# First context, its keys, values and queries of layer one's cross attention, and first rows, made inside the preceding stages of a decoder kernel

## What is computed

```python
# layer zero's experts, whose result enters layer one
return x + _mlp(x, shared_wg, shared_wu, shared_wd) + expert_weighted
# layer one, self attention
qkv = (X @ W_qkv).reshape(b, s, h, d, 3)
weights = softmax(q @ k.T / sqrt(64))
out = (weights @ v).reshape(b, s, h * d) @ W_out
# layer one, cross attention
xn, cn = layer_norm(x, g1, b1), layer_norm(context, g2, b2)
q = xn @ Wq
k, v = split(cn @ Wkv)
out = softmax(q @ k.T * 64**-0.5) @ v @ Wout + bout
```

## Time and profile before

| | |
|---|---|
| runs, median (lowest to highest) | 1822.67 us (1822.57 to 1828.09) |
| the profiled execution's own time | 1826.97 us, of it 1825.3 us span |
| TensorE busy in the span | 1645.2 us, 90% |
| VectorE, ScalarE, GpSimd busy | 61%, 49%, 31% |
| stage experts_0 ends, self_attention_1 begins | about 722 to 727 us in the span |
| stage self_attention_1 ends, context_attention_1 begins | about 1070 to 1071 us |
| stage context_attention_1 ends | about 1480 us |

### The profile page before, as it was taken

How to read it: one execution, slowest core, us unless ns; L and a number is a source line. 1 busy time by engine, 2 the same in 40 slices (tenths; PEclk the granted TensorE clock), 3 DMA queues, 4 the chain that set the end, 5 groups by cost and what they waited for, 6 DMA issues and landing times. The chain is left out here.

```text
span 1825.3 us, 36539 instructions
## 1 busy us (share of the span) xinstructions
PE 1645.2 (90%) x12703; PEld 1360.2 (75%) x12703; DVE 1118.3 (61%) x2667; ACT 885.8 (49%) x2544; POOL 558.4 (31%) x864
## 2 busy tenths in 40 slices
PE   5997599999998887599999869999999989999998
PEld 3665467777776576488888757777777779999987
DVE  4776467777777433377776645667666554444464
ACT  2333255555555133155555524444444456666644
POOL 2112222444443234322221121222332256444410
PEclk8999699999999799799999979999999989999999
DMA  8000323444450353100000020000000032213001
GB/s 252 0 0 1 117 78 119 129 127 127 127 169 12 130 167 118 44 14 14 17 12 1 1 87 19 17 18 18 18 18 1 1 127 82 70 70 137 2 1 41
DMA packets 87277, 114.29 MB, mean 63 GB/s; under 512 B 4788, under 2 KB 76680, under 8 KB 86888
## 3 DMA queue, kind: packets, MB, share of 16 engines
q1 hardware_dynamic: 82008, 99.56, 16.9%
q0 software_dynamic: 5136, 12.98, 2.1%
HBM read 64.68 MB, written 47.84 MB: 62 GB/s over the span
## 5 line engine op out<-in xcount | busy, mean ns | idle before, releaser
L1029 ACT ACTIVATE c_probs<-ps,c_negmax 112x375 f32<-112x375 f32 x256 | 143.7, 581 | 2.1 <-DVE c_negmax L1135 2.1
L1240 PEld LDWEIGHTS ps<-const,c_probs 112*125 112x125 f32 x768 | 97.8, 193 | 47.3 <-DVE c_pT L1157 27.5
L1135 DVE TENSOR_REDUCE c_negmax<-ps 112x2 f32<-112x750 f32 x128 | 114.2, 934 | 25.7 <-PE ps L1271 25.7
L1240 PE MATMUL ps<-const,c_probs 112*125 112x112 f32 x768 | 116.1, 289 | 3.6 <-ACT c_probs L1029 2.4
L1988 PE MATMUL ps<-xnT,s_qkv 128*128 128x224 f32 x512 | 112.7, 370 | 4.6 <-ACT e_gate_up L1777 4.1
L1793 ACT ACTIVATE s_probs<-ps,s_negmax 112x112 f32<-112x112 f32 x256 | 86.7, 364 | 36.4 <-DVE s_negmax L1851 36.4
L1988 PEld LDWEIGHTS ps<-xnT,s_qkv 128*128 128x128 f32 x512 | 96.3, 196 | 10.8 <-ACT e_gate_up L1777 5.7
L1330 PE MATMUL ps<-parts 128*125 128x256 f32 (+1 forms) x480 | 91.0, 327 | 5.5 <-DVE X L1086 2.4
L2903 DVE TENSOR_TENSOR e_hid_low<-xnT,e_hid_high 128x528 fp32r<-128x528 f32 x56 | 41.1, 733 | 83.5 <-ACT e_hid_high L2803 83.5
L1017 ACT COPY c_pT<-ps 125x672 f32<-125x672 f32 x64 | 46.1, 720 | 82.1 <-PE ps L1240 82.1
L1330 PEld LDWEIGHTS ps<-parts 128*125 128x125 f32 (+1 forms) x480 | 71.7, 196 | 13.0 <-DVE c_kT L1081 4.4
(11 more groups left out here) (473 smaller groups left out, 5088.1 us busy)
## 6 DMA issues: line engine op xcount, KB each, us to landing
expert_rows<-d_zero SPq DMA_DIRECT2D x16, 2240.0 KB
c_ctx_in<-in_ctx SPq DMA_DIRECT2D x32, 375.0 KB
e_x_in<-expert_rows SPq DMA_DIRECT2D x43, 128.0 KB, 2.1
expert_rows<-e_y POOLq DMA_DIRECT2D x43, 128.0 KB, 2.1
e_w_gate_even<-in_L_ffn_w_gate SPq DMA_DIRECT2D x4, 1024.0 KB, 5.1
e_w_fc_even<-in_L_ffn_w_c_fc SPq DMA_DIRECT2D x4, 1024.0 KB, 7.3
e_w_proj_even<-in_L_ffn_w_c_proj SPq DMA_DIRECT2D x4, 1024.0 KB, 9.8
c_kv<-in_L_ffn_w_gate SPq DMA_DIRECT2D x4, 1024.0 KB, 5.0
```

The source lines that it names most:

```text
L1029: last = nc.scalar.activation(probs[:, g % 2, r, :], ps[:T, r, 0:S], ACT.Exp, bias=negmax[:, par, h:h + 1], accum_out=sums[:, par, h:h + 1])
L1135: nc.vector.tensor_reduce(negmax[:, par, h:h + 3:2], ps[:T, 2 * piece:2 * piece + 2, 0:S], AX.X, ALU.max, negate=True).then_inc(max_done, 1)
L1240: last = nc.tensor.transpose(ps[:KC, bank + r % 2, k * T:(k + 1) * T], probs[:, g % 2, r, k * KC:(k + 1) * KC], ident[:T, :T])
```

## The change

- A class `Wide` cuts tiles out of one memory of 8192 float32 per partition that lives from the start to the end of layer one's cross attention. Six tiles of `linear_attention` with `attnT`, three of `context_attention_0`, the weights of `self_attention_1` (queries and keys apart from values now) and the keys, values, transposed context and first queries of `context_attention_1` take turns in it.
- In `experts_0`: SyncE loads context 0 after the other loads; VectorE normalises it in ten small steps, one per tile j of 28 to 37, GpSimd takes its power at j of 33; TensorE transposes it before the last two steps; behind the last step it makes the keys of sequence 0 (8 products of 128 x 375) and the first of three value parts (2 products of 512 columns), in plain float32 instead of split products. ScalarE and VectorE copy them out. GpSimd, not SyncE, waits for all stores, and then issues the gathers of sequences 0 and 1.
- In `self_attention_1`: TensorE makes the two other value parts of context 0 first; the gathers go without a copy of the row numbers; sequence q's sum is made one iteration earlier (0 and 1 both in iteration -5), with two sets of norm tiles; contexts 1 and 2 are loaded when four sums were made; context 1, not 0, is normalised in the iterations B-3 and B-2; in the last iteration TensorE makes the first queries of the next stage (8 products of 224 columns) and ScalarE copies them out.
- In `context_attention_1`: the scores, maxima and exponentials of sequence 0 stand ahead of the iterations; the contexts, keys and values of 0 and the queries of the first pair are gone from them. Context 3 is loaded once context 1 is normalised, which it is at the start.

The diff, cut:

```diff
+class Wide:
+
+
+    SIZE = 8192
+
+    def __init__(self, memory):
+        self.memory, self.at = memory, 0
+
+    def afresh(self):
+        self.at = 0
+        return self
+
+    def __call__(self, shape):
+        n = int(np.prod(shape[1:]))
+        assert self.at + n <= self.SIZE
+        flat, self.at = self.memory[:shape[0], self.at:self.at + n], self.at + n
+        names = "abcd"[:len(shape) - 1]
+        return flat.rearrange("p (" + " ".join(names) + ") -> p " + " ".join(names), **dict(zip(names, shape[1:])))
...
-        w = sb("wqkv", [128, 2, 3 * D])
+        wide = sh.wide
+        w = wide([128, 2, 3 * D])
...
-        kT = sb("kT", [128, 2, 2, S])
-        v = sb("v", [KC, 2, NK, VROW])
-        probs = sb("probs", [T, 2, GROUPS, S])
+        wide = sh.wide.afresh()
+        kT = wide([128, 2, 2, S])
+        v = wide([KC, 2, NK, VROW])
+        probs = wide([T, 2, GROUPS, S])
...
+def gather_rows(nc, sh, w, q, u):
+
+    for k in range(2):
+        nc.gpsimd.indirect_dma_start(out=w.gathered[:, u, k, :], out_offset=None, in_=sh.xs[:, :],
+                                     in_offset=bass.IndirectOffsetOnAxis(ap=sh.kept_row[:, q, k:k + 1], axis=0)).then_inc(w.arrived[u], 16)
...
+                if j == LATER + len(later):
+                    entry.load(sp, 0, 0)
...
+                if j == CONTEXT_AT + 5:
+                    entry.power(pool, 0)
+            for u in range(IN_SLOTS):
+                pool.wait_ge(stored[u], (BLOCKS - u + IN_SLOTS - 1) // IN_SLOTS * 16)
+            pool.sem_inc(passed, 1)
+            for q in range(2):
+                gather_rows(nc, sh, following, q, q)
...
+            for m in (1, 3):
+                act.wait_ge(early_mm, m + 1)
+                nc.scalar.copy(later_w.kT[0][:, m, :], ps[:, KEY_BANKS[m], 0:S]).then_inc(early_taken, 1)
...
+                if 0 <= j - CONTEXT_AT < entry.STEPS:
+                    entry.step(dve, 0, 0, j - CONTEXT_AT)
...
+            dve.wait_ge(following.parts_ready, 16)
+            for c in range(2):
+                dve.wait_ge(ctx_mm, c + 1)
+                nc.vector.tensor_scalar(later_w.ctxT[:, c, :], ps[:, BANK_X + c, 0:S], sh.columns[:, 148 + c:149 + c],
+                                        sh.columns[:, 150 + c:151 + c], ALU.mult, ALU.add).then_inc(ctxT_ready, 1)
+            for m in (0, 2):
+                dve.wait_ge(early_mm, m + 1)
+                nc.vector.tensor_copy(later_w.kT[0][:, m, :], ps[:, KEY_BANKS[m], 0:S])
+            dve.wait_ge(early_mm, 5)
+            nc.vector.tensor_copy(later_w.v[0][:, 0, :], ps[:KC, BANK_X, :])
...
+                if j == LAST - 1:
+                    pe.wait_ge(entry.cn_ready, 1)
+                    pe.wait_ge(xT_ready, BLOCKS)
+                    for c in range(2):
+                        for k in range(NK):
+                            last = nc.tensor.transpose(ps[:, BANK_X + c, k * KC:(k + 1) * KC], entry.cn[:, k, c * 128:(c + 1) * 128], ident[:KC, :KC])
+                        last.then_inc(ctx_mm, 1)
+            pe.wait_ge(sh.w_loaded["c1"], 64)
+            pe.wait_ge(ctxT_ready, 2)
+            for m in range(4):
+                for c in range(2):
+                    last = nc.tensor.matmul(ps[:, KEY_BANKS[m], 0:S], later_w.kv[:, c, m * 128:(m + 1) * 128], later_w.ctxT[:, c, :],
+                                            start=(c == 0), stop=(c == 1))
+                last.then_inc(early_mm, 1)
+            for c in range(2):
+                last = nc.tensor.matmul(ps[:KC, BANK_X, :], later_w.ctxT[:, c, 0:KC], later_w.kv[:, c, 512:1024], start=(c == 0), stop=(c == 1))
+            last.then_inc(early_mm, 1)
...
+    STEPS = 10
+
+    def step(self, dve, q, u, n):
+        nc = self.nc
+        if n < NK:
+            if n == 0:
+                dve.wait_ge(self.loaded[u], q * 8 + 16 - 8 * u)
+                dve.sem_inc(self.passed, 1)
+            last = nc.vector.bn_stats(self.stats[:, n, :], self.ctx_in[:, u, n, :])
+            if n == NK - 1:
+                last.then_inc(self.chain, 1)
+        elif n == NK:
+            dve.wait_ge(self.chain, q * 2 + 1)
+            dve.sem_inc(self.passed, 1)
+            for j in range(NK):
+                last = nc.vector.bn_aggr(self.mv[:, j, :], self.stats[:, j, :])
+            last.then_inc(self.chain, 1)
+        elif n == NK + 1:
+            dve.wait_ge(self.chain, q * 2 + 2)
+            nc.vector.tensor_scalar(self.veps[:, :], self.mv[:, :, 1], LN_EPS, None, ALU.add).then_inc(self.var_ready, 1)
+        elif n >= self.STEPS - NK:
+            j = n - self.STEPS + NK
+            if j == 0:
+                dve.wait_ge(self.rstd_ready, q + 1)
+            last = nc.vector.tensor_scalar(self.cn[:, j, :], self.ctx_in[:, u, j, :], self.mv[:, j, 0:1],
+                                           self.rstd[:, j:j + 1], ALU.subtract, ALU.mult)
+            if j == NK - 1:
+                last.then_inc(self.cn_ready, 1)
...
+        def sums_at(i):
+
+            if i <= -AHEAD:
+                return range(2) if i == -AHEAD - 1 else ()
+            return (i + AHEAD + 1,) if within(i + AHEAD + 1) else ()
...
-            for u in range(2):
-                entry.load(sp, u, u)
+            sp.wait_ge(taken, AHEAD)
+            for q in (1, 2):
+                entry.load(sp, q, q % 2)
...
-                if not (isinstance(q, int) and q < 2):
-                    pool.wait_ge(taken, q - 1)
+                pool.wait_ge(taken, q - 1)
                 pool.sem_inc(passed_in, 1)
-                nc.gpsimd.tensor_copy(row[:, u, :], sh.kept_row[:, q, :]).then_inc(row_ready, 1)
-                pool.wait_ge(row_ready, q + 1)
-                pool.sem_inc(passed_in, 1)
-                for k in range(2):
-                    nc.gpsimd.indirect_dma_start(out=gathered[:, u, k, :], out_offset=None, in_=sh.xs[:, :],
-                                                 in_offset=bass.IndirectOffsetOnAxis(ap=row[:, u, k:k + 1], axis=0)).then_inc(arrived[u], 16)
+                gather_rows(nc, sh, w, q, u)
...
-                gather(i + AHEAD + 2, par)
+                gather(i + AHEAD + 3, 1 - par)
                 if i == B - 2:
-                    entry.power(pool, 0)
+                    entry.power(pool, 1)
...
+                if i == B:
+                    for half in range(2):
+                        act.wait_ge(query_mm, half + 1)
+                        nc.scalar.copy(later_w.qT[0][:, :, 2 * half:2 * half + 2, :].rearrange("p s m t -> p m s t"),
+                                       columns_of(ps[:, BANK_S + half, :]))
...
+            for k in range(1, NK):
+                act.wait_ge(early_mm, k)
+                nc.scalar.copy(later_w.v[0][:, k, :], ps[:KC, BANK_O + k - 1, :])
...
-                entry_sum(i, par)
+                if i >= 0:
+                    for q in sums_at(i):
+                        entry_sum(q)
...
+                if i < 0:
+                    for q in sums_at(i):
+                        entry_sum(q)
...
+            def later_queries():
+                pe.wait_ge(exp_done, 4 * B)
+                for half in range(2):
+                    for m in range(2):
+                        cols = slice((2 * half + m) * 128, (2 * half + m + 1) * 128)
+                        for c in range(2):
+                            last = nc.tensor.matmul(ps[:, BANK_S + half, 2 * m * T:2 * (m + 1) * T], later_w.q[:, c, cols],
+                                                    sh.xnT[:, c, 0:2, :].rearrange("p s t -> p (s t)"), start=(c == 0), stop=(c == 1))
+                    last.then_inc(query_mm, 1)
...
+                if i == B:
+                    later_queries()
...
+            for k in range(1, NK):
+                for c in range(2):
+                    last = nc.tensor.matmul(ps[:KC, BANK_O + k - 1, :], later_w.ctxT[:, c, k * KC:(k + 1) * KC], later_w.kv[:, c, 512:1024],
+                                            start=(c == 0), stop=(c == 1))
+                last.then_inc(early_mm, 1)
...
-    side = Side([("slots0", -3, ON_ACT), ("result", -1, ON_DVE), ("query", 2, ON_ACT), ("key0", 1, ON_DVE), ("context0", 2, ON_ACT),
-                 ("key1", 1, ON_DVE), ("key2", 1, ON_ACT), ("slots1", -3, ON_ACT),
-                 ("key3", 1, ON_DVE), ("rows_ranks", -1, ON_DVE, B + 1), ("value0", 1, ON_ACT), ("value1", 1, ON_DVE),
-                 ("context1", 2, ON_ACT), ("inverse_logits", 0, ON_DVE, B + 1), ("value2", 1, ON_ACT)])
+    side = Side([("slots0", -3, ON_ACT), ("result", -1, ON_DVE), ("query", 2, ON_ACT, B, 2), ("key0", 1, ON_DVE, B, 1), ("context0", 2, ON_ACT, B, 1),
+                 ("key1", 1, ON_DVE, B, 1), ("key2", 1, ON_ACT, B, 1), ("slots1", -3, ON_ACT),
+                 ("key3", 1, ON_DVE, B, 1), ("rows_ranks", -1, ON_DVE, B + 1), ("value0", 1, ON_ACT, B, 1), ("value1", 1, ON_DVE, B, 1),
+                 ("context1", 2, ON_ACT, B, 1), ("inverse_logits", 0, ON_DVE, B + 1), ("value2", 1, ON_ACT, B, 1)])
...
+            sp.wait_ge(cn_ready, 2)
```

(23 more changed lines are left out.)

203 lines of the change are left out of this document (106 added, 97 removed).

## The result

| | kernel before | changed kernel |
|---|---|---|
| median of the runs beside each other | 1825.38 us (4 runs, 1822.57 to 1828.60) | 1811.07 us (4 runs, 1809.45 to 1811.88) |
| ratio | | 0.9925, 95% interval 0.9908 to 0.9942 |
| the same comparison repeated | 1825.01 us (11 runs) | 1809.41 us (6 runs), 0.9917, 0.9902 to 0.9932 |
| profiled execution, span | 1826.97 us, 1825.3 | 1809.45 us, 1807.8 |

The change makes the kernel faster by 14 to 16 us. The forecast was 1804.5 us with a range up to 1811: the sign is right, the time is not. Two things are to be found: what the forecast's 18.2 us really were, and how much of the gap is the starting point of the sum.

What follows compares the result with a forecast made beforehand. TensorE was taken as the bound inside stages, so only two stage borders could gain: 14.8 and 3.4 us make 18.2, and 1822.67 less 18.2 gives 1804.5 us, range 1799 to 1811 us.

Steps and rivals of the forecast that it cites:

- starting point: Whole kernel: the time before the change, taken as a median of 1822.67 us, from which 18.2 us were subtracted.
- B: Border self_attention_1 to context_attention_1: scores start at once, the old order is reached earlier; gain 14.8 us, bounds 12 to 17.
- A: Border experts_0 to self_attention_1: second transposes follow sooner and less half clock; gain 3.4 us, bounds -1 to 7.
- ten VectorE steps ... hidden; at worst 0.3 each where the power is late: Tile loop of experts_0: steps fit VectorE's idle time; with six context transposes 0.6 us, bounds 0 to 3.
- With the barrier the next one starts at 732.9: End of experts_0: gathers end at 731.2, the barrier adds some 1.7 us, then self_attention_1 starts.
- the value products: Start of self_attention_1: two value parts on TensorE take 3.9 us at full clock, 7.6 at half.
- gathers: End of experts_0: GpSimd issues four gathers, 1.3 us each, from 726.0 to 731.2.
- keys and values: End of experts_0: TensorE's ten products take 5.7 and 1.9 us, from 722.0 to 729.6.
- rival 3: Border into context_attention_1: context 3 lands late and VectorE stands for 5 us; 1809.5 us, chance 0.04.
- rival 5: Self_attention_1 and context_attention_0: new addresses in the wide memory slow TensorE's products; 1829 us at 3.5%, chance 0.03.
- rival 4: Start of context_attention_1: the removed 22.9 us return as waits of iteration 0; 1819 us or more, chance 0.04.
- The rule weighed: Experts_0: VectorE and GpSimd share memory interfaces, so stores come later beside the new steps; gain 1 us smaller.

Runs made afterwards that it cites:

- queries_back: Changed kernel with the first queries of context_attention_1 made at that stage's start again, not inside self_attention_1: 1812.9 us (6 runs).
- power_early: Changed kernel with GpSimd's root of the first context's variances taken one tile earlier: 1804.3 us (10 runs, together with its repeat).
- gather_split: Changed kernel with only sequence 1's gathers moved from the end of experts_0 to the start of self_attention_1: 1810.9 us (6 runs).
- gather_late: Changed kernel with the gathers of sequences 0 and 1 moved from the end of experts_0 to the start of self_attention_1: 1810.6 us (6 runs).
- sums_early: Changed kernel with GpSimd's root one tile earlier and the sums of sequences 0 and 1 moved to the end of experts_0: 1804.9 us (4 runs).
- power_again: The same kernel as power_early, run once more: 1804.3 us (10 runs, both together).
- keys_back: Changed kernel with the first context's keys and first values made at the start of self_attention_1, not the end of experts_0: 1817.3 us (10 runs).

## Why the prediction was wrong, step by step

- **The starting point** (1822.67 us). The median of three runs stood for that of the kernel, and I took 4.3 us off a profiled execution that lay 1.8 above the median of 41. This made the forecast 2.5 us low. From 1825.1 the same sum gives 1806.9, inside 2.7 us of the changed kernel's 1809.6. The four runs of the result lie another 1.5 us above that.
- **B, 14.8 us.** Right, as sum and as mechanism; 7.1 us of it are shown by undoing (queries_back), the rest by rows. The distance from the barrier to the second head's transposes was 28.3 us (four traces) and is 12.3 (three): 16.0 for 15.8. Later in the stage 1.2 us of them are given back, where I had taken off 1 for the clock.
- **A, 3.4 us: 0.8.** In three parts: experts_0 up to the last expert product went from 100.4 to 104.9 us, +4.5 where I had +0.6; the border from 45.4 to 41.5, -4.0 where I had -4.0 (3.4 and the 0.6); from the first scores to the end of the stage 302.9 to 301.5, -1.4, which no step had.
- **The step that failed** is "ten VectorE steps ... hidden; at worst 0.3 each where the power is late". I looked at VectorE's idle time per tile and not at GpSimd's queue: at this tile GpSimd reads the tile table for 2.4 us, then stores, then takes the root, and so comes when VectorE already stands before the next tile's work. 1.87 us, shown by power_early; that the table read makes it late is read from the rows and was not undone by itself. The bound of 3 us held it; the value taken didn't. The rest of the +4.5 is the half-clock stretch (1.66 us, two of three traces) and scatter ahead of these tiles (81.0 us in the mean of three against 79.5 in four).
- **The border came out right by two errors.** "With the barrier the next one starts at 732.9" took 1.7 us behind the last gather for what takes 5.0: 3.3 us missing. The 4.72 us of the earlier trace rows had been split into 1.7 for the barrier and 3.0 for the store's landing; the landing took 1.4, and GpSimd's drain holds the barrier. Against it, the value products ran 5.35 us, not 7.6, since the clock rose during them, and the pieces began 7.5 us behind the stage's start, not 10.0; and they began at full clock, where I had allowed for half of the loss. The first-scores distance from the first piece fell from 22.8 to 20.3 us.
- Details that held: gathers at 728.8 to 733.55, 4.75 us for a forecast 5.2; keys and values 7.0 us for 7.6; context 3 without a wait (rival 3); products of 224 columns at 1.78 us for eight records in the border, and 361 ns each in the stage where they were 370 (rival 5); no waits that take B's place (rival 4).
- The rule weighed, that VectorE and GpSimd hinder each other: in the tile loop no distance shows it. With the root moved "tiles" is 20.90 us as before, with six VectorE steps more. In context_attention_1 single rows do: a context step of VectorE beside GpSimd's arithmetic took 0.85 us in the changed kernel (at 1077.22), the two behind it 0.40 each. The Trainium skill (DMA: Bandwidth & Descriptors, SWDGE vs HWDGE vs iDMA) states the lock for VectorE's 2-port mode only, a condition that the prediction left out; no row here tells the mode.

## What to carry to other kernels

A step that is spread over the idle time of one engine has to be looked up in the queues of all the engines that it passes: here one GpSimd instruction, placed behind its queue's own read of a table, cost 1.9 us, and moving it by one tile gave that back. The late store could be seen in the trace of the kernel before. Work moved ahead of a barrier is free only up to what ends the stage; where that is GpSimd's gathers and its drain, everything that lies beside them is free (the keys: 7.8 us), and work left right behind the barrier can be worth more than it costs, because it brings TensorE's clock up before the long chain begins. And take the starting point from as many runs as there are, and stage lengths from more than one trace: a stretch at half clock costs 1.7 us a time, and the one trace was 3.6 us above the mean of four in the very place of the change.

## What the runs showed of the hardware

- GpSimd's own drain at the end of a stage ended 4.1 us behind the end of its last gather's issue (eleven traces; 3.9 in gather_split), 3.75 us behind that of its last store (kernel before, four traces), and took 3.7 us where its stores had landed before it began (gather_late). Behind GpSimd's last arithmetic at border B it ended 2.4 us later (changed kernel, 1065.5 and 1067.8). The barrier's drain came 0.3 us behind it in all of these but gather_late. The gathered rows were readable 1.8 us behind the last issue (sums_early).
- GpSimd's read of the tile table took 2.36 to 2.41 us at tile 33 (kernel before, changed kernel, power_early), and in the changed kernel the store behind it came 1.7 us late, which the timeline's bracket puts down to ScalarE.
- The granted clock of one kernel at one place differs between executions: 24.4 or 22.8 us for the same 14 tiles of the changed kernel, and value products of 5.29 and 6.62 us behind the same barrier in power_early and power_again, which are one kernel. Stretches of this kind are a large part of what differs between traces of one kernel; its totals spread over 8.0 us (kernel before, eleven runs) to 11.2 us (keys_back, ten runs).
- After the gap at this border the clock rose 2.8 to 6.1 us into TensorE's next unbroken work (eleven traces of the changed kernel and its variants in which it stood at half when that work began); in the kernel before, whose work there had gaps of up to 3.79 us, it stayed at half until 744 to 752.
